# GpSimd's block inversion one slot later, norms and decay factors ahead of the output's scale, and the normed output with its transposition later in the slot

## The reference

```python
qkvz = hidden_states @ W_qkvz; ba = hidden_states @ W_ba
...
y = silu(causal depthwise convolution of q, k, v, 4 taps)
q = jnp.repeat(_l2norm(q), KV_RATIO, axis=2) * DK ** (-0.5)
k = jnp.repeat(_l2norm(k), KV_RATIO, axis=2)
def step(S, inp):
    qt, kt, vt, gt, bt = inp
    S = S * jnp.exp(gt)[:, None, None]
    kv = jnp.einsum('hk,hkv->hv', kt, S)
    delta = (vt - kv) * bt[:, None]
    S = S + kt[:, :, None] * delta[:, None, :]
    return (S, jnp.einsum('hk,hkv->hv', qt, S))
...
gated = core * jax.nn.silu(z)
gated = gated * jax.lax.rsqrt(jnp.mean(gated * gated, axis=-1, keepdims=True) + EPS)
return (gated * norm_w).reshape(B, Tn, VDIM) @ W_out
```

## Time and profile before

| | us |
|---|---|
| median of 3 runs | 3036.22 |
| lowest, highest | 3026.62, 3046.79 |
| the profiled execution | 3028.94 |
| its span | 3027.2 |
| TensorE busy | 2794.9 |
| VectorE busy | 2181.0 |
| ScalarE busy | 1812.3 |
| GpSimd busy | 1565.5 |

### The profile page before, as it was taken

The page is one execution under the profiler, slowest core; times in us unless marked ns, Lnnn a source line. Parts: engine busy times, 40 slices in busy tenths (PEclk is TensorE's granted clock), DMA queues, the critical chain, the costliest instruction groups (busy, mean ns, idle before and its releaser), DMA issues. The chain is left out here.

```text
span 3027.2 us, 75586 instructions
## 1 busy us (share of the span) xinstructions
PE 2794.9 (92%) x24303; PEld 1909.6 (63%) x24303; DVE 2181.0 (72%) x4677; ACT 1812.3 (60%) x6310; POOL 1565.5 (52%) x3737
## 2 busy tenths in 40 slices
PE   5999489999999999999999999999999999869998
PEld 4556256666666666666666666666666666655555
DVE  3443468878877887877778778877788788547676
ACT  3321557777766776777677667766677677332332
POOL 1000456667666666666667666766666666410000
PEclk9999789999999999999999999999999999979999
DMA  3000132212222222212122212122222222110000
GB/s 88 1 1 0 28 59 40 45 38 45 42 48 43 49 43 44 49 35 49 35 49 42 54 37 51 39 46 38 45 40 52 42 49 42 24 42 1 8 7 15
DMA packets 485567, 113.74 MB, mean 38 GB/s; under 512 B 423296, under 2 KB 484336, under 8 KB 485168
## 3 DMA queue, kind: packets, MB, share of 16 engines
q1 hardware_dynamic: 485168, 108.76, 18.0%
HBM read 80.63 MB, written 28.06 MB: 36 GB/s over the span
## 5 line engine op out<-in xcount | busy, mean ns | idle before, releaser
L1216 DVE SCALAR_TENSOR_TENSOR S<-S,gs,bank 128x128 f32<-128x128 f32 x1024 | 287.3, 343 | 232.3 <-PE bank L776 228.0
L1247 DVE SCALAR_TENSOR_TENSOR conv<-raw,ckq,conv 128x512 f32<-128x512 f32 x384 | 302.2, 799 | 110.4 <-ACT conv L1001 104.1
L539 POOL TENSOR_TENSOR btmp<-Bk,Tb 64x14 f32<-64x14 f32 (+6 forms) x896 | 339.7, 379 | 66.1 <-POOL Tb L543 0.9
L543 POOL TENSOR_TENSOR Tb<-Tb,btmp 64x14 f32<-64x14 f32 (+6 forms) x896 | 315.2, 352 | 70.9 <-POOL btmp L539 1.3
L986 ACT ACTIVATE sq_gat<-gat 128x128 bf16<-128x128 f32 x512 | 151.8, 297 | 279.2 <-DVE gat L1232 279.2
L1247 DVE SCALAR_TENSOR_TENSOR conv<-raw,cv,conv 128x512 f32<-128x512 f32 x384 | 291.6, 772 | 12.2 <-ACT conv L1001 7.3
L528 POOL TENSOR_TENSOR Tb<-Bk,lower 64x256 f32<-64x256 f32 x64 | 56.0, 875 | 434.8 <-issue 429.0
L1020 ACT ACTIVATE gatn<-gat,ty 128x128 f32<-128x128 f32 x512 | 163.5, 390 | 181.3 <-POOL ty L518 181.3
L733 PE MATMUL bank<-xnT,wkq 128*128 128x512 f32 x512 | 255.8, 623 | 11.6 <-POOL mkX L425 10.7
L749 PE MATMUL bank<-wz_h,xnT 128*128 128x256 f32 x1024 | 260.6, 401 | 0.0
L819 PE MATMUL bank<-wout_h,gT 128*128 128x256 f32 x1024 | 257.0, 394 | 0.0
(11 more groups left out here) (354 smaller groups left out, 6660.1 us busy)
## 6 DMA issues: line engine op xcount, KB each, us to landing
rowb<-decay_rows SPq DMA_DIRECT2D x256, 64.0 KB, 3.9
blk_n<-N SPq DMA_DIRECT2D x256, 64.0 KB, 2.5
Tp<-blk_t SPq DMA_DIRECT2D x128, 128.0 KB, 2.9
Wp<-blk_w SPq DMA_DIRECT2D x128, 128.0 KB, 3.0
wkq<-in_L_attn_W_qkvz_dram SPq DMA_DIRECT2D x32, 128.0 KB, 2.3
wv<-in_L_attn_W_qkvz_dram SPq DMA_DIRECT2D x16, 256.0 KB, 3.6
Bk<-blk_n SPq DMA_DIRECT2D x64, 64.0 KB, 2.6
blk_t<-Tb SPq DMA_DIRECT2D x64, 64.0 KB, 2.5
```

Of the source, the lines that this page charges most:

```text
L539: pool.tensor_tensor(tmp, Bk[:, j, j + 1:].unsqueeze(2).broadcast_to([64, 15 - j, j]), Tb[:, j, 0:j].unsqueeze(1).broadcast_to([64, 15 - j ...
L543: pool.tensor_tensor(Tb[:, j + 1:, 0:j], Tb[:, j + 1:, 0:j], tmp, ALU.subtract).then_inc(row_rdy, 1)
L1216: i = dve.scalar_tensor_tensor(out=S[:, 2 * b + v, :], in0=S[:, 2 * b + v, :], scalar=gs[t.c][:, kind, 2 * h + v:2 * h + v + 1], in1=pKU[b ...
L1247: dve.scalar_tensor_tensor(out=y, in0=raw[h][:, j, :, :, k:k + H].rearrange("p c b n -> p (c b) n"), scalar=cw[:, j, k:k + 1], in1=y, op0= ...
```

## The change

Six edits, all of order:
1. GpSimd's `base_first` works on step s-3 instead of s-2, `base_rest` on the pair of step s-5 instead of s-4: both one slot later. `base_out` on SyncE moves with `base_rest` and now stands behind `dump` in its slot. `x16` is not moved.
2. GpSimd runs `out_scale` behind `derive`, `scaled` and `causal`.
3. ScalarE runs `norms` ahead of `squares`.
4. ScalarE runs `normed` behind `from_state(s, 1)`, so `evac(s, 0)`, `clamp`, `expo` and `evac(s, 1)` go ahead of it.
5. TensorE runs `gated_tp` behind `zproj`.
6. In `base_start`, register values for waits are computed ahead of the first wait.

The last three hunks are the bodies of GpSimd, TensorE and ScalarE; the one with `dump` is SyncE's.

```diff
                 def base_out(s):
-                    t = s.back(4)
+                    t = s.back(S_F + 3)
...
                     value_weights(s)
+                    dump(s)
                     base_out(s)
-                    dump(s)
...
                 def base_start(t):
-                    read, sent = held(pool, t.pairs(16, 16)), held(pool, t.pairs(16))
+                    read, sent, begun, ones = (held(pool, v) for v in (
+                        t.pairs(16, 16), t.pairs(16), t.pairs(2, 1), t.pairs(2, 2)))
...
-                    pool.wait_ge(base_in, t.pairs(2, 1))
+                    pool.wait_ge(base_in, begun)
...
-                    pool.wait_ge(base_in, t.pairs(2, 2))
+                    pool.wait_ge(base_in, ones)
...
                 def base_first(s):
-                    t = s.back(S_F)
+                    t = s.back(S_F + 1)
...
                 def base_rest(s):
-                    t = s.back(4)
+                    t = s.back(S_F + 3)
...
                 def body(s):
                     step_gates(s)
                     halo(s)
-                    out_scale(s)
                     derive(s)
                     scaled(s)
                     causal(s)
+                    out_scale(s)
                     base_rest(s)
                     base_first(s)
...
                     values(s)
+                    zproj(s)
                     gated_tp(s)
-                    zproj(s)
                     low_rank(s)
...
                 def body(s):
+                    norms(s)
                     squares(s)
-                    norms(s)
                     from_state(s, 0)
                     kdec(s)
-                    normed(s)
                     evac(s, 0)
                     clamp(s)
                     expo(s)
                     evac(s, 1)
                     from_state(s, 1)
+                    normed(s)
                     vscale(s)
```

## The result

The changed kernel took **3333.35 us** (median of 4 runs, 3328.72 to 3334.45); the kernel before took 3031.42 beside it (4 runs, 3016.51 to 3046.79). The ratio is **1.0993, interval 1.0934 to 1.1051**: slower, 33 us above the forecast of 3300 and inside its range. The profiled execution took 3328.72 us, its span 3327.0, at a mean granted clock of 0.923 of full speed (0.971 before).

What follows compares the result with a forecast made beforehand. TensorE, busy 92%, lost 119 us to gaps, nearly all in even slots, through GpSimd's late base_first. Waits and clock +336, weights +38, ends +10, less 119, gave +265: 3300 us, range 3120 to 3400.

Steps and rivals of the forecast that it cites:

- The main term: TensorE before x16 in every even slot: waits 4.0 us for the late inverted block Tp, 59 times.
- The collision with y's silu: GpSimd's first chain instruction takes 1.26 us beside VectorE's silu; without that the chain is 1.0 us shorter.
- The clock: TensorE after each pause before x16: slower granted clock costs another 1.7 us, in 59 even slots.
- More is late: Rival at x16: pauses of 5.6 us with 2.65 of slow clock each, +416, 3450 us; chance 0.08.
- the clock stays up: Rival: x16's wait costs no clock, +165, 3200 us; chance 0.19 together with the short chain.
- The weights: SyncE's queue: base_out holds up the next head's wkq and ckq, another 2.7 us at 14 changes of head.
- The term of -119: TensorE's whole gap before solve(s, 1), nearly all in even slots, goes: 119 us won.
- The road I had followed: Late base_first delays out_scale, then ScalarE's normed and evac(s, 0), VectorE's taps, rhs(s, 1) and TensorE's solve(s, 1).
- The cover of the normed output: TensorE's transposition of normed's output comes at 12.5, normed ends near 11.3: 1.2 us of cover, costed at nothing.
- The ends: Drain and fill of the pipeline, outside the 119 slots: two or three more such waits, +10 us estimated.
- Tp comes in time, faster: Rival at x16: GpSimd's chain runs ahead of TensorE, the gain of 119 is whole, 2917 us; chance 0.08.

Runs made afterwards that it cites:

- e2: Kernel before with edits 1 and 6 alone (inversion one slot later, base_out behind dump): 3328.97 us, ratio 1.1031.
- e5: Changed kernel with rows 6 to 9 of the block inversion moved from base_rest to base_first: 3096.94 us, ratio 1.0248.
- e9: Changed kernel with inversion rows 1 to 11 in base_first, 12 to 14 in base_rest, and next head's weights issued ahead of base_out: 2958.18 us, 0.9796.
- e3: Changed kernel with SyncE issuing the next head's wkq and ckq ahead of base_out: 3265.53 us, ratio 1.0818.
- e4: Changed kernel with 14 unused 128x128 matmuls ahead of x16's wait in even slots: 3248.80 us, ratio 1.0746.
- e1: Changed kernel with GpSimd's inversion and SyncE's base_out put back in their old slots (edits 2 to 6 alone): 3053.55 us, ratio 1.0102.
- e8: Kernel before with edits 4 and 5 alone (normed behind from_state(s, 1), gated_tp behind zproj): 3015.08 us, ratio 0.998.
- e11: Kernel before with edits 2 and 3 alone (out_scale behind causal, norms ahead of squares): 3494.12 us, ratio 1.1581.
- e12: e9 with the load of Bk between base_out's writes and reads, and the mask and rows 1 to 3 ahead of derive in even slots: 2927.39 us, 0.9694.
- e6: Changed kernel with inversion rows 6 to 9 moved to base_first and next head's weights issued ahead of base_out: 3030.86 us, ratio 1.0038.

## Why the prediction was right

**The main term, 59 waits of 4.0 us (236): held, 243.7 measured.** The chain came as worked out: derive at 1.93 (1.85 forecast), Tb at 16.28 (16.68), reads 2.52 behind the write (2.56), Tp at 22.5 (22.85). The collision with y's silu stayed, as argued: derive's first instruction took 1.13 us, where the same one took 0.23 behind the silu in the trace before (1540.22). The wait is 3.94 in ordinary even slots, 4.74 in those that start a head, 4.13 on average. e2 shows that the shift alone makes it, e5 and e9 that it goes down with the rows in the odd slot.

**The clock, 59 x 1.7 (100): right mechanism, too small.** 98.3 us in the 45 ordinary slots, and 29.0 in the 14 others by e3's slow part, together 127, or 2.2 a slot. No run shows 1.7 for waits of 4.0; the changed kernel showed these 2.2. The 1.7 is the mean over eight pauses before solve(s, 1) in the trace before, seven of 3.10 to 3.98 us and one of 2.84. From L764 to the next increment their slots took 1.52, 2.71, 1.73, 1.72, 2.65, 1.73, 0.05 and 1.74 us more than the 3.29 of the odd slot (1528.24 to 1531.53), 1.73 on average. The fifth is the pause of 3.39 there (granted clock 0.50), the seventh the one of 3.10, with the clock at 1.00 behind it. The 2.65 is also what "More is late" counted for each pause. Of the 45 slots here 44 lost 1.4 to 3.0 us and one lost nothing. The pauses are longer than most of those behind the mean, but whether that is what makes them dearer is not shown: among the 45 a wait of 3.64 lost 2.95 and one of 4.44 lost 1.44. e4 shows that this is the clock (8.2 us in the 45 slots without the idleness, for 98.3). The rival "the clock stays up" falls with it.

**The weights, 14 x 2.7 (38): the size held, its make-up only in part.** e3 has 40.8. But TensorE's wait for ckq is 1.9 us a head and not 2.7; the other 1.0 is the longer slow stretch, which the sum did not have. That the two together come near 2.7 is luck.

**The term of -119: the size held, the reason was half wrong.** In the 119 slots almost nothing of the old pause is left (243.7 + 127.3 + 40.8 is 411.8 of 414.3). But I put it down to two things, that base_first's wait goes and that derive and normed leave their places. e2 shows that the first suffices; e1, with the second alone, kept the pause, e8 had no effect, and e11 made it worse. The road I had followed (out_scale, normed, evac) was one of several: halo and ETn are others. The step that was wrong is the sentence "Behind `normed` in ScalarE's queue is evac(s, 0)" taken as the only way.

**The cover of the normed output: held.** gatn ends 11.1 us into its slot (11.3 forecast), its transposition stands at 12.4, odd slots take 16.90.

**The ends**: 4.5 us instead of 10. In all the span grew by 300 where 265 was forecast, and the clock's term is 27 of the 35 missing (the waits are 8 more, the weights 3, the rest of the slots 2.5, the ends 5.5 less).

**"Tp comes in time, faster"** was the right rival to fear: it needed the chain 2.8 us shorter, and e9 and e12 are that case, at 2958 and 2927 us. The forecast for it was 2917.

## What to carry to other kernels

When a step moves one slot later to be rid of its wait, count the slot starts that lie between it and its first reader, and follow its chain (here norms, GpSimd, a write and a read through DRAM) in microseconds against the reader's place: two slots had hidden what one does not. If the chain is too long by a little, move rows of it into the idle stretch before it and put loads into the gaps of its queue, and see which instructions of the other engines it will then stand beside. Before crediting a reordering with a pause, look for every engine that waits on the late one, since with one road closed the pause can stay whole on the next, as in e1. And cost an instruction by what it stands beside: a row taken out of the chain here saved its undisturbed duration, and the stretch beside VectorE's taps passed to the row that came in its place (e6: rows that had taken 4.1 us gave 2.6).

## What the runs showed of the hardware

- A pause of some 3.9 us in dense matmuls cost 2.2 us more on average (1.4 to 3.0 in 44 of 45 cases, nothing in one); in the slot shown the granted clock went from 1.00 to 0.50 within the pause of 3.57 us and was back 6.3 us after the matmuls began again. With matmuls filling 3.4 us of the pause (e4) it cost 0.2, and the clock stayed at 1.00 in the slot shown. With a second idleness of 2.78 us inside the slow stretch (head slot from 1716.07) the clock was at 0.50 for about 10 us, 1721.7 to 1731.9.
- GpSimd's small instructions stretched beside VectorE's taps (scalar_tensor_tensor, 128x512): the same 64x14 product took 0.20 us ahead of them (e12) and 0.68 beside them (e6). The stretch stayed with the taps: the two rows that stood there took 2.72 us in the changed kernel and 2.76 in e6, against 1.1 for rows of the first sizes in e9 (1996.24 to 1997.59) and 0.86 for those of the second in e12. That is why e6 gained 2.6 us and not 4.1.
